# Moving the small arithmetic of four normalizations from GpSimd to VectorE

## The reference

```
ln(x)  = (x - mean) / sqrt(var + 1e-5)
r      = ln(x);  rn = r * rsqrt(mean(r*r) + 1e-5) * norm_w
skip   = rn @ W_skip;  u = silu(conv4(rn @ W_in) + conv_b)
delta  = softplus(u @ W1 @ W2 + b);  B, C = u @ W_B, u @ W_C
h_l    = h_(l-1) * exp(delta_l * A) + delta_l * u_l * B_l;  y_l = sum_n h_l * C_l
x1     = x + ln(r + ((y + u*W_D) * silu(skip)) @ W_out)
f      = ln(x1);  s = softmax(f @ router + bias);  top 8 of 64
out    = x1 + ln(f * sum(top8) + top8 @ expert_bias)
```

## Time and profile before

| what | us |
|---|---|
| median of 3 runs (lowest, highest) | 2184.91 (2182.64, 2185.52) |
| the profiled execution, time | 2178.91 |
| the profiled execution, span in the profile | 2177.1 |
| mean granted TensorE clock, share of full | 0.961 |
| busy: PE, DVE, ACT, POOL | 1893.4, 1726.6, 1716.2, 1859.3 |

### The profile page before, as it was taken

The page is one execution under the profiler, slowest core; times in us unless marked ns, Lnnn a source line. Parts: engine busy times, 40 slices in busy tenths (PEclk is TensorE's granted clock), DMA queues, the critical chain, the costliest instruction groups (busy, mean ns, idle before and its releaser), DMA issues.

```text
span 2177.1 us, 35466 instructions
## 1 busy us (share of the span) xinstructions
PE 1893.4 (87%) x12005; PEld 1585.3 (73%) x12005; DVE 1726.6 (79%) x2529; ACT 1716.2 (79%) x3404; POOL 1859.3 (85%) x1256
## 2 busy tenths in 40 slices
PE   5677777999999998999999898999989898989883
PEld 4566767878787786878778786978778686767551
DVE  3487878898898989888888988888898978888332
ACT  3489797979888897979889897988889798888221
POOL 1299999899999999999999999999989899999312
PEclk9999898999999999999999999999999999999995
DMA  5656566765766575765756585765757464645310
GB/s 174 209 189 212 184 212 206 241 215 190 242 201 223 170 265 175 245 220 184 253 177 228 186 269 177 226 227 183 250 162 250 149 229 166 218 151 184 116 49 20
DMA packets 234672, 425.92 MB, mean 196 GB/s; under 512 B 18623, under 2 KB 134907, under 8 KB 234491
## 3 DMA queue, kind: packets, MB, share of 16 engines
q1 hardware_dynamic: 234490, 423.65, 59.0%
HBM read 339.18 MB, written 84.41 MB: 195 GB/s over the span
## 4 chain that ended last, share of the span: by engine, by line
PE 31%; POOL 16%; DVE 15%; ACT 10%; issue 7%; DMA 7%; DVEq 0%; SPq 0%; POOLq 0%; ACTq 0%
DVE h L971 10%; POOL hc L613 9%; PE mixed L1363 6%; PE bank L1152 6%; PE y_sum L1157 6%; PE pair_bank L1283 4%; DMA c_all<-bc_dram 4%; ACT u_t L747 3%; PE routed L1337 3%; POOL operand L597 2%; DVE hv L1034 2%; ACT operand L728 2%; DMA dx_q<-dx_dram 2%; PE routed L1237 1%; DMA dx_dram<-dx 1%
## 5 line engine op out<-in xcount | busy, mean ns | idle before, releaser
L613 POOL TENSOR_TENSOR hc<-h,c_all 128x1024 f32<-128x1024 f32 x512 | 1205.0, 2367 | 83.0 <-DVE h L971 76.0
L971 DVE TENSOR_TENSOR_SCAN h<-operand,carry,bank 128x512 f32<-128x512 f32 x528 | 649.2, 1266 | 126.1 <-PE bank L1152 112.7
L747 ACT ACTIVATE u_t<-dx_t,lbc 128x256 f32<-128x256 f32 x1408 | 631.8, 498 | 19.0 <-PE bank L1152 18.9
L1157 PE MATMUL y_sum<-ident,hc 128*128 128x128 f32 x4096 | 601.6, 278 | 7.5 <-POOL hc L613 6.8
L1152 PE MATMUL bank<-ident,u_t 128*128 128x128 f32 x2816 | 448.6, 284 | 165.5 <-DVE h L971 162.6
L1152 PEld LDWEIGHTS bank<-ident,u_t 128*128 128x128 f32 x2816 | 336.3, 145 | 274.1 <-issue 176.3
L1157 PEld LDWEIGHTS y_sum<-ident,hc 128*128 128x128 f32 x4096 | 490.7, 144 | 47.1 <-issue 27.5
L728 ACT ACTIVATE operand<-delta_q,neg_a 128x512 f32<-128x512 f32 x704 | 480.0, 711 | 0.0
L597 POOL TENSOR_TENSOR operand<-dx_q,b_all 128x1024 f32<-128x1024 f32 x160 | 378.4, 2365 | 8.4 <-DMA b_all<-bc_dram 8.4
L728 ACT ACTIVATE bank<-delta_q,neg_a 128x512 f32<-128x512 f32 x320 | 218.1, 682 | 204.1 <-DVE h L971 203.7
L971 DVE TENSOR_TENSOR_SCAN h<-bank,carry,operand 128x512 f32<-128x512 f32 x240 | 295.8, 1268 | 27.4 <-POOL operand L597 17.0
(11 more groups left out here) (119 smaller groups left out, 1858.5 us busy)
## 6 DMA issues: line engine op xcount, KB each, us to landing
c_all<-bc_dram SPq DMA_DIRECT2D x256, 512.0 KB, 4.3
b_all<-bc_dram SPq DMA_DIRECT2D x160, 256.0 KB, 5.5
win<-in_L_attn_W_in SPq DMA_DIRECT2D x64, 512.0 KB, 6.0
wskip<-in_L_attn_W_skip SPq DMA_DIRECT2D x64, 512.0 KB, 6.5
x_dram<-x SPq DMA_DIRECT2D x64, 256.0 KB, 6.2
delta_dram<-delta SPq DMA_DIRECT2D x32, 512.0 KB, 7.6
dx_dram<-dx SPq DMA_DIRECT2D x32, 512.0 KB, 5.3
delta_q<-delta_dram SPq DMA_DIRECT2D x32, 512.0 KB, 5.9
```

Of the source, the lines that this page charges most:

```text
L613: nc.gpsimd.tensor_tensor(hc[:, number % 3], h[:, number % 3], c_all[:, j % 2, s % 2:s % 2 + 1].to_broadcast([P, 2, SPAN]), ALU.mult).then ...
L747: last = nc.scalar.activation(u_t[:, j % 2, b], dx_t[:, k, b], ACT.Copy, scale=lbc[:, stage % 2, b, DELTA + n:DELTA + n + 1])
L971: nc.vector.tensor_tensor_scan(h[:, number % 3, q], first, second, start, ALU.mult, ALU.add).then_inc(scan_done.sem, 1)
L1157: return matmul(to, lhsT=of, rhs=ident[:], is_transpose=True, start=start, stop=stop, skip_group_check=True)
```

## The change

GpSimd keeps the power alone, once per normalization. The two powers of the first one become one on a tile of 128x4: with v the variance, the product of the two rstd is the power of v(1 + eps) + eps squared. VectorE makes everything else, with three new forms: a tensor by constants (`tensor_scalar`), a product of two tensors, and minus mean times rstd in one instruction.

| normalization | GpSimd before | GpSimd after | VectorE after, besides the moments |
|---|---|---|---|
| x | 11 in slots -4, -3, -1 | 1 (128x4), slot -4 | 2 in slot -8, 1 (128x4) in slot -2 |
| z | 4 in slot 15 | 1, slot 14 | 1 in slot 13, 1 in slot 15 |
| h | 4 in slot 22 | 1, slot 21 | 1 in slot 20, 1 in slot 22 |
| o | 7 in slot 42 | 1, slot 42 | 3 in slot 41, 2 in slot 43 |

The moments of o move from slot 41 to slot 40. The last aggregate of every `moments` is now waited for before the next instruction.

```diff
+                def rsqrt(to, of, halves):
+                    return nc.gpsimd.tensor_tensor(to, of, halves, ALU.pow)
...
-                            if "norm" in jobs_now:
-                                now = kept[:, (FIRST + t + 3) % KEPT]
-                                if s == -4:
...
-                                    link(rstd(now[:, 2], small["varx"][:], mvx[:, :, 1]))
-                                    link(times(small["ms"][:], mvx[:, :, 1], now[:, 2]))
-                                if s == -3:
-                                    link(times(small["ms"][:], small["ms"][:], now[:, 2]))
-                                    link(rstd(small["r2"][:], small["ms"][:], small["ms"][:]))
-                                if s == -1:
-                                    link(times(now[:, 0], now[:, 2], small["r2"][:]))
-                                    minus_mean_times(now[:, 3], mvx, now[:, 2])
-                                    minus_mean_times(now[:, 1], mvx, now[:, 0]).then_inc(s_ready.sem, 1)
+                            if "norm" in jobs_now and s == -4:
...
+                                rsqrt(kept[:, (FIRST + t + 3) % KEPT, 0:2], both_varx, mhalf[:]).then_inc(r_ready.sem, 1)
...
-                                if s == 15:
+                                if s == 14:
...
-                                    link(rstd(small["rz"][:], small["varz"][:], mvz[:, :, 1]))
-                                    minus_mean_times(small["nz"][:], mvz, small["rz"][:]).then_inc(nz_ready.sem, 1)
+                                    rsqrt(small["rz"][:], small["varz"][:], mhalf[:, 0]).then_inc(rz_ready.sem, 1)
...
+                def times(to, a, b):
+                    return nc.vector.tensor_tensor(to, a, b, ALU.mult)
+
+                def and_eps(to, var):
+                    return nc.vector.tensor_scalar(to, var, EPS, None, ALU.add)
+
+                def minus_mean_times(to, mean, r):
+                    return nc.vector.scalar_tensor_tensor(out=to, in0=mean, scalar=-1.0, in1=r, op0=ALU.mult,
+                                                          op1=ALU.mult)
...
+                                moments(xn, mvx)
+
+                                and_eps(small["varx2"][:], mvx[:, :, 1])
+                                nc.vector.tensor_scalar(small["varx"][:], mvx[:, :, 1], 1 + EPS, EPS * EPS, ALU.mult,
+                                                        ALU.add).then_inc(var_x.sem, 1)
+                            if "norm" in jobs_now and s == -2:
...
+                                minus_mean_times(now[:, 2:4], mvx[:, :, 0].unsqueeze(1).to_broadcast([P, 2, TB]),
+                                                 now[:, 0:2]).then_inc(s_ready.sem, 1)
...
-                                if s == 41:
+                                rs, var, ro = small["rs"][:], small["varo"][:], small["ro"][:]
+                                if s == 40:
                                     if v := due(dve, o_ready, t, TB):
                                         dve.wait_ge(o_ready.sem, v)
-                                    moments(o, mvo, var_o)
+                                    moments(o, mvo)
+                                if s == 41:
+                                    link(times(var, mvo[:, :, 1], rs))
+                                    link(times(var, var, rs))
+                                    and_eps(var, var).then_inc(var_o.sem, 1)
+                                if s == 43:
+                                    if v := due(dve, ro_ready, t, 1):
+                                        dve.wait_ge(ro_ready.sem, v)
+                                    link(times(ro, ro, rs))
+                                    minus_mean_times(small["no"][:], mvo[:, :, 0], ro).then_inc(no_ready.sem, 1)
```

More of the change, by code:

```diff
@@ L220, in build @@
         x_loaded = loads_of("x_loaded", "norm", 1)
-        var_x, s_ready = signal("var_x", "norm", 1), signal("s_ready", "norm", 1)
+        var_x, r_ready, s_ready = (signal(n, "norm", 1) for n in ("var_x", "r_ready", "s_ready"))
         rn_ready = signal("rn_ready", "norm", TB)
@@ L253, in build @@
         eb_done, o_ready = signal("eb_done", "route", TB), signal("o_ready", "route", TB)
-        var_o, no_ready = signal("var_o", "route", 1), signal("no_ready", "route", 1)
+        var_o, ro_ready, no_ready = (signal(n, "route", 1) for n in ("var_o", "ro_ready", "no_ready"))
         on_ready, out_ready = signal("on_ready", "route", TB), signal("out_ready", "route", 1)
@@ L690, in _ @@
                                         pool.wait_ge(var_o.sem, v)
[L691 to L698 removed]
+                                    rsqrt(small["ro"][:], small["varo"][:], mhalf[:, 0]).then_inc(ro_ready.sem, 1)
                                 if s == 45:
@@ L942, in copied, with moments @@
                     return nc.vector.tensor_reduce(to, of.unsqueeze(len(of.shape)), axis=AX.X, op=ALU.add)
-                def moments(of, mv, ready):
+                def times(to, a, b):
[5 more added lines that the diff above has]
+                                                          op1=ALU.mult)
+                def moments(of, mv):
                     for b in range(TB):
@@ L949, in moments @@
                         last = nc.vector.bn_aggr(mv[:, b], stat6[:, b])
-                    last.then_inc(ready.sem, 1)
+                    link(last)
                 def scan(t, s):
@@ L1003, in _ @@
                                     dve.wait_ge(s_ready.sem, v)
-                                moments(xn, mvx, var_x)
+                                moments(xn, mvx)
[3 more added lines that the diff above has]
+                            if "norm" in jobs_now and s == -2:
+                                if v := due(dve, r_ready, t, 1):
+                                    dve.wait_ge(r_ready.sem, v)
+                                now = kept[:, (i + 3) % KEPT]
+                                minus_mean_times(now[:, 2:4], mvx[:, :, 0].unsqueeze(1).to_broadcast([P, 2, TB]),
+                                                 now[:, 0:2]).then_inc(s_ready.sem, 1)
                             if "prep" in jobs_now:
@@ L1086, in _ @@
                                         dve.wait_ge(z_ready.sem, v)
-                                    for read in (nz_ready, var_o):
-                                        if v := due(dve, read, t - 1, 1):
-                                            dve.wait_ge(read.sem, v)
-                                    moments(z, mvz, var_z)
+                                    moments(z, mvz)
+                                    and_eps(small["varz"][:], mvz[:, :, 1]).then_inc(var_z.sem, 1)
+                                if s == 15:
+                                    if v := due(dve, rz_ready, t, 1):
+                                        dve.wait_ge(rz_ready.sem, v)
+                                    minus_mean_times(small["nz"][:], mvz[:, :, 0], small["rz"][:]).then_inc(nz_ready.sem, 1)
                                 if s == 20:
@@ L1093, in _ @@
                                         dve.wait_ge(x1_ready.sem, v)
-                                    if v := due(dve, nh_ready, t - 1, 1):
-                                        dve.wait_ge(nh_ready.sem, v)
-                                    moments(x1, mvh, var_h)
+                                    moments(x1, mvh)
+                                    and_eps(small["varh"][:], mvh[:, :, 1]).then_inc(var_h.sem, 1)
+                                if s == 22:
+                                    if v := due(dve, rh_ready, t, 1):
+                                        dve.wait_ge(rh_ready.sem, v)
+                                    minus_mean_times(small["nh"][:], mvh[:, :, 0], small["rh"][:]).then_inc(nh_ready.sem, 1)
                                 if s == 32:
```

32 lines of the change are left out of this document (13 added, 19 removed).

## The result

The changed kernel takes 2259.8 us (median of 4 runs, 2255.6 to 2263.3) against 2185.2 (2182.6 to 2189.5): ratio 1.035, 95% interval 1.033 to 1.037. It is 74.6 us slower; the prediction said 33 slower, and its range ended 1.8 us short. The profiled execution took 2255.6 us, with a span of 2253.8, 76.7 over the one before.

What follows compares the result with a forecast made beforehand. GpSimd was taken to bound both ends, with VectorE setting the pace in slots 7 to 14 of middle steps; 2178.9 - 11 + 39 + 3 + 2, stated as 2212.9, plus 6.0 for the median, given as 2218 us; 8-in-10 range 2164 to 2258.

Steps and rivals of the forecast that it cites:

- The interlock: VectorE's small SBUF instructions beside a busy GpSimd wait for GpSimd's instruction in flight, up to 2.37 us.
- the upper bound of the two: Cost of one small VectorE instruction beside GpSimd: between nothing and GpSimd's instruction in flight, up to 2.37 us; the latter taken.
- o, 39 us: Output norm, slots 9 and 11: waits for GpSimd cost 3.9 us per o in steps 4 to 13, 39 us.
- The ends, -11 us: Steps 0 to 2 and the last stretch, GpSimd-bound: late scans absorbed by its backlog, 11 of 17.0 us saving kept.
- The other waits, 3 us in the middle: Waits of z, h and x: 1.2 us each in the mean against a cover of 0.9, 0.3 per step.
- 3.6 not kept: h's part on the chain before the store of `dx` in four middle steps: saving 4 x 0.9 us, none kept.
- The saving: GpSimd's relief where it counts, both ends and h's part in four middle steps: 20.6 us in all.
- The first rival: VectorE reads without waiting, so GpSimd's saving comes through: 2168 us, faster by 0.75%; chance 0.28.
- The queue after the last scan: `thg` waits behind the output sum and z's power: +2.0 us in each of two rounds, last round gains 2, sum +2.
- the 6.2 us a chunk: GpSimd time saved per chunk over all four norms, 99 us for 16 chunks if GpSimd alone set the time.
- blocked for the whole instruction: Shared SBUF port of VectorE and GpSimd: whichever comes second waits until the other's instruction ends.

Runs made afterwards that it cites:

- dummy_one: Kernel before the change plus 12 spare VectorE instructions a step in the change's slots, as one-input tensor_reduce on [128x2]: 2192.9 us, ratio 1.004.
- dummy_two: Kernel before the change plus 12 spare VectorE instructions a step in the change's slots, as SBUF-to-SBUF tensor_scalar and tensor_tensor on [128x2]: 2249.0 us, ratio 1.031.
- columns: Changed kernel with VectorE's small instructions split into one-column tensor_scalar instructions, the second factor given as a pointer: 2165.2 us, ratio 0.991.
- o_two: As columns, but the output norm's five small instructions in the changed kernel's two-column forms: 2215.4 us, ratio 1.014.
- ends_pointer: Changed kernel with one-column pointer forms up to scan step 2 and from scan step 14 on, two-column forms in steps 3 to 13: 2225.4 us, ratio 1.018.
- middle_pointer: Changed kernel with one-column pointer forms in scan steps 3 to 13 only, two-column forms at the ends: 2206.4 us, ratio 1.010.
- grouped: Kernel before the change with x's two powers made in one [128x4] instruction and its shifts in one product, all on GpSimd: 2178.4 us, ratio 0.9975.
- columns_tt: As columns, but the one-column products take two tensor operands instead of a pointer: 2252.3 us, ratio 1.031.
- dummy_three: As dummy_two, but with each spare instruction on [128x3] instead of [128x2]: 2253.8 us, ratio 1.032.

## Why the prediction was right in kind and wrong in size

**The interlock: right.** It took the upper bound of the two for a small instruction beside `hc`. The rows at 1263.98 and 1273.40, 0.15 us after the last scan, and dummy_one against dummy_two show it. But the reason given covered `tensor_scalar` only by likeness; it held at two and three columns and not at one.

**o, 39 us: near in the middle, left out at the ends.** From scan 8 to the moments of z the middle steps grew by 3.9 us, as said. But 0.7 of it is there in columns too (24.4), which has the instructions without the waits, so that the waits are worth 3.3 a step; o_two shows 33.6 us of span in steps 3 to 13. In steps 14 and 15, for which the prediction counted no wait of o, the same stretch grew from 20.9 to 26.7 us, by more than in the middle, and o_two has 13.6 us over columns from step 14 on. By medians o costs 50.3.

**The ends, -11 us: the step that failed.** "In the POOL-bound ends a late scan is absorbed while GpSimd works off its backlog": it kept 11 of 17.0 us, a loss of 6. ends_pointer shows a loss of 34.4 (of which the 2 us of `thg` aren't part, since it keeps that wait). Steps 0 to 2 together grew by 9.6 us with just three new instructions each, step 14 by 7.7, step 15 and the rest by 9.1; each of these steps should have been shorter by 1 to 3. The backlog is no cover for this kind of wait, because it is the backlog that keeps VectorE out: when the small instruction gets in, the backlog is gone (the rows of step 1), and GpSimd runs dry. GpSimd stood idle for 1.6 and 3.1 us in steps 14 and 15 before, 11.3 and 12.6 after, and 0.9 and 3.8 in ends_pointer. In steps 0 to 2 the kernels with the waits there (after, middle_pointer) have 9.6 and 8.3 us over the one before, and those without (columns, ends_pointer, o_two) 6.1 to 8.7 under it. The loss of 34.4 in place of 6 makes 28 of the 42 us by which the prediction fell short.

**The other waits, 3 us in the middle: too small.** middle_pointer gives 53.4 us for steps 3 to 13, where the prediction had 39 + 3 and 3.6 not kept, 45.6. In the spans, after less columns is 50.6 there, and less o's 33.6 leaves 17, 1.5 a step in place of 0.3, though single executions are good to some 7 us only. The 0.9 us waits for TensorE cover these only partly. In numbers of waiting: o's instructions last 66.9 us in o_two and would last 12.8 at 0.16 each, 54 us of waiting for 50.3 of time, 0.93 to one. All of the new ones last 176.5 in after, 31 without waiting, 145 us for 94.6; what is not o's, 91 us for 44, 0.5 to one. dummy_two's 138 us cost 56, 0.4 to one. So what a wait costs per microsecond differs by more than twice; o's share was measured with the other waits gone.

**The saving: right in size, not shown in place.** The first rival had 2168 for the case that VectorE reads without waiting; columns, with the change's whole relief of GpSimd and no wait, takes 2165.2. It supports the -20.6, against which columns' own 26 instructions a step stand. Where it lies isn't shown: grouped got 5.3 us of the 10 that a like reckoning gave it, and the spans place only 5.8 of columns' 18.6 us.

**The queue after the last scan: right in order.** `thg` starts behind L680, as said. From the start of the last `hc` to the end of the span are 157.3 us, 155.5 before: +1.8, where +2 was said. But the same stretch takes 160.4 in columns, which has no long instruction there, so the agreement may be luck.

**Smaller terms.** GpSimd's busy time fell by 70.6, not 95: the 6.2 us a chunk held the gaps between linked instructions, which aren't busy time. The [128x4] power takes 1.015 us, not 1.22, so two more columns cost 0.31. Middle steps take 127.5 us (steps 3 to 12: 465.62 to 1741.07), as said; but by the same measure they took 122.7 before (458.68 to 1685.79) and not 123.5, so that they grew by 4.8 each. The terms of the sum add up to 2211.9 and 2217.9, not to the 2212.9 and 2218.9 that it states; the 2218 that was given agrees with them.

What stays open is why the waits of z, h and x cost a half of their length in the mean; no run parts them. Nor does one part what the lower clock adds: TensorE's 12005 instructions take 32.8 us more at 0.944 of the clock than at 0.961 before, and columns, without the waits, has 1892.9 us at 0.961 again. How much of the 94.6 us goes through the clock isn't shown.

## What to carry to other kernels

Before a small operation moves from GpSimd to VectorE, look at its form, not its size: a [128x2] product of two SBUF tensors lasted 1.2 to 1.8 us in the mean in three of its places beside a GpSimd that was 80% busy, and as two one-column instructions with a pointer 0.4 together. That form for all of the new ones turned +3.5% into -0.9%. Don't count on an engine's backlog to cover a wait for that engine's own instructions: here it was worked off while the other waited. And where the same tiny instruction has a mean of ten times its shortest, the profile's busy time hides a wait; look at which instruction of another engine ends at the same time, here to some hundredths of a microsecond.

## What the runs showed that was not expected

One VectorE instruction was kept out over two GpSimd instructions in a row (3.58 us, where an `hc` takes 2.37); dummy_two's longest is 3.865, that of columns_tt 4.64.

The power didn't keep VectorE out where they met. In dummy_two the spare product of slot 15, with two SBUF inputs, ran to its end in 0.13 us inside a power of 0.71; VectorE, then GpSimd:

```profile
916.51 0.13 DVE L949 TENSOR_TENSOR spare<-mhalf 128x2 f32<-128x2 f32 x1
```

```profile
916.40 0.71 POOL L577 TENSOR_TENSOR stats<-stats,mhalf 128x2 f32<-128x2 f32 x1
```

There are 7 such cases in dummy_two and 9 in dummy_three, and in neither run nor in after does a long VectorE instruction end with a power. So "blocked for the whole instruction", as the prediction has it, fits the [128x1024] instructions and not this one.

`tensor_scalar` with a pointer takes 205 to 207 ns on one column, with constants 146 to 149, a price that only the pointer makes. The new product of slot 15 never waited for GpSimd's use of SBUF (138 ns in the mean of 16): in the 13 steps with a scan VectorE comes to it right behind the scan for which GpSimd itself is waiting.
